# Key norm factors of a cross-attention kernel: turned as two f16 halves and spread over the score layout by a 0/1 matrix, in place of f32 transposes of widened factors

## What is computed

```python
q = (hidden_states @ Wq).reshape(B, Sq, H, D)
k = (encoder_hidden_states @ Wk).reshape(B, Skv, H, D)
v = (encoder_hidden_states @ Wv).reshape(B, Skv, H, D)
q = rmsnorm(q, gq)
k = rmsnorm(k, gk)          # k * rsqrt(mean(k*k) + eps) * gk
scores = jnp.einsum('bqhd,bkhd->bhqk', q, k) * scale
attn = jax.nn.softmax(scores, axis=-1)
out = jnp.einsum('bhqk,bkhd->bqhd', attn, v)
return out.reshape(B, Sq, H * D) @ Wo
```

## Time and profile before

| | |
|---|---|
| median of three runs | 1506.91 us |
| profiled execution | 1508.46 us |
| its span in the trace | 1506.6 us |
| DVE, ACT busy | 987.6 us (66%), 837.5 us (56%) |
| granted TensorE clock, mean | 0.933 |
| DMA | 59.65 MB, mean 40 GB/s |

### The profile page before, as it was taken

One profiled execution on the slowest core, in us unless ns is written; L12 is line 12 of the kernel. 1 busy time (PEld: TensorE's weight loads), 2 busy tenths in 40 slices (PEclk: granted clock), 3 DMA queues, 4 the chain that ended last, 5 costly groups with the idle time before them and its releaser, 6 DMA issues.

```text
span 1506.6 us, 35628 instructions
## 1 busy us (share of the span) xinstructions
PE 1297.3 (86%) x10526; PEld 874.2 (58%) x10526; DVE 987.6 (66%) x3748; ACT 837.5 (56%) x3560; POOL 531.6 (35%) x1337
## 2 busy tenths in 40 slices
PE   5877898999999999989898989899999999955881
PEld 2554565666666666665656656566666666634661
DVE  6754777777677777776767676777767777732212
ACT  4445575747475757566566657575747575711110
POOL 2044152525252533435352515252535243310004
PEclk9998999999999999999999999999999999876996
DMA  9000010101010100000000000010101011002344
GB/s 370 31 23 15 9 30 11 32 11 32 11 32 11 33 11 29 11 26 18 22 21 22 21 8 29 11 32 11 32 11 32 11 32 39 31 3 75 120 153 126
DMA packets 41191, 59.65 MB, mean 40 GB/s; under 512 B 5094, under 2 KB 35953, under 8 KB 40096
## 3 DMA queue, kind: packets, MB, share of 16 engines
q1 hardware_dynamic: 36880, 50.73, 10.6%
q0 software_dynamic: 2064, 6.14, 1.2%
q10 hardware_dynamic: 2176, 2.10, 0.4%
HBM read 48.62 MB, written 10.49 MB: 39 GB/s over the span
## 4 chain that ended last, share of the span: by engine, by line
PE 49%; DVE 21%; issue 9%; POOL 8%; DMA 3%; ACT 3%; POOLq 0%; DVEq 0%; SPq 0%; ACTq 0%
PE AB L594 25%; PE Db L594 9%; PE Eb L594 5%; POOL prob L1177 4%; PE C L719 4%; PE C L594 3%; DVE kst L1312 3%; DVE rq L1360 2%; DMA ctxn<-expert_rows 2%; DVE nc_ L1284 2%; DVE nc_ L1285 2%; DVE nb_ L1286 1%; PE C L787 1%; DVE prob L1471 1%; PE C L734 1%
## 5 line engine op out<-in xcount | busy, mean ns | idle before, releaser
L950 ACT ACTIVATE AB<-AB 128x128 f32<-128x128 f32 (+1 forms) x1160 | 305.3, 263 | 172.8 <-PE AB L594 168.3
L1132 POOL TENSOR_TENSOR pjunk<-pjunk 128x1 f32<-128x1 f32 x288 | 56.1, 195 | 748.4 <-DVE sinv L1482 431.3
L1312 DVE BATCH_NORM_STATS2 kst<-AB 128x6 f32<-128x256 f32 x512 | 181.8, 417 | 68.1 <-PE AB L594 63.0
L950 ACT ACTIVATION_READ_ACCUMULATOR AB<-AB 128x1 f32 (+1 forms) x1160 | 217.3, 187 | 0.0
L594 PE MATMUL AB<-wk_hi,c_hi 128*128 128x512 f16 x512 | 203.7, 398 | 11.9 <-DVE smax L1471 2.9
L594 PE MATMUL AB<-wk_lo,c_hi 128*128 128x512 f16 x512 | 201.3, 393 | 0.0
L594 PE MATMUL AB<-wk_hi,c_lo 128*128 128x512 f16 x512 | 199.7, 390 | 0.0
L1020 ACT ACTIVATE prob<-prob,nbias,rq 128x257 f32<-128x257 f32 x256 | 150.6, 592 | 7.9 <-DVE nbias L1477 7.9
L1177 POOL TENSOR_SCALAR prob<-prob,sinv 128x257 f32<-128x257 f32 x256 | 123.4, 482 | 20.2
L594 PE MATMUL AB<-ctxT,qpT 128*128 128x257 f32 x512 | 124.0, 385 | 0.0
L594 PEld LDWEIGHTS AB<-wk_hi,c_hi 128*128 128x128 f16 x512 | 52.2, 102 | 94.7 <-issue 25.2
(11 more groups left out here) (252 smaller groups left out, 2923.8 us busy)
## 6 DMA issues: line engine op xcount, KB each, us to landing
ctxT<-in_ctxT SPq DMA_DIRECT2D x64, 128.5 KB, 2.1
...
```

Source lines behind the costliest of these rows:

```text
L950: ins = nc.scalar.activation(k, k, ACT.Square, accum_out=sums[0:m, h:h + 1])
L1132: own.mark(pool.tensor_tensor(pjunk[:, 0:1], pjunk[:, 1:2], pjunk[:, 1:2], ALU.mult))
L1312: ins = V.bn_stats(stats[:, 0, 2 * half + n], AB[0:m, 2 + half, 2 * D * n:2 * D * (n + 1)])
```

## The change

The wide buffer `rkx` goes. POOL's new step R_k (k = 0, 1; `split_rk`) waits for KN_k and writes the 64 factors of each context row as an f16 half and the rest as a second f16 half, into `rk16`. PE's new step rt_k (`turn_rk`) turns each of the two blocks by one f16 product with the f16 identity: 64 columns in (sequence, half, head) become 64 partitions. ACT copies them (256 columns) into `rkT`. PE's rk_b is now four products of `spread16[:, b % 2]`, a 64 x 512 matrix of zeros and ones, with `rkT`: both halves are added and every head lands on its 32 partitions. ACT's copy into `rkb` stays. POOL's r_b writes the last column only. `spread16` is built by two DVE operations in step `low` of the first tile. The first tile's one-time widening (`step_rkl`) uses the buffer `sc`; the ternary weights' load and one of the final buffers, which had lain in `rkx`, have other places (`wt_in` of its own, `wvo_words`). The lists of steps change: R and rt come in, and other steps change places as well.

```diff
-    "PE": """K0 pt3 K1 X K2 o3 K3 f Q xt1 rk0 qkv K4 QP s0 qk sc rk1 K5 K6 K7 pv pt0 s1 st pr rk2 s2 o0 xt2 rk3
-              lg up s3 pt1 dn pos o1 pt2 o2""".split(),
-    "ACT": """K0 tl3 K1 X ph3 K2 oh3 K3 Q xt1 rk0 qkv K4 QP qk e0 K5 sc K6 K7 rk1 pv tl0 ph0 rk2 e1 oh0 xt2 rk3 up
-              e2 lg ph1 tl1 e3 oh1 ph2 tl2 oh2""".split(),
-    "DVE": """K0 X K1 XL dp3 K2 do3 K3 KN0 f Q RQ K4 qkv s0 sc i0 K5 sm K6 K7 KN1 ys dp0 yv s1 pr ln2 i1 s2 lg do0
-              up s3 i2 dp1 dn pos do1 dp2 i3 do2""".split(),
-    "POOL": """h0 n3 h3 h1 X c0 cl r1 h2 ln1 c3 r0 n0 c2 r2 c1 y r3 ln2 n1 n2 scat""".split(),
+    "PE": """K0 pt3 K1 X K2 o3 K3 f Q rt0 xt1 rk0 qkv K4 QP s0 qk sc rk1 K5 K6 K7 pv pt0 s1 st rt1 pr rk2 s2 o0
+              xt2 rk3 s3 up lg pt1 dn pos o1 pt2 o2""".split(),
+    "ACT": """K0 ph3 K1 X tl3 K2 oh3 K3 Q rt0 xt1 rk0 qkv K4 QP qk e0 K5 sc K6 K7 rk1 pv ph0 tl0 rt1 rk2 e1 oh0
+              xt2 rk3 up e2 ph1 tl1 lg e3 oh1 ph2 tl2 oh2""".split(),
+    "DVE": """K0 X K1 dp3 XL K2 do3 K3 KN0 f Q RQ K4 qkv s0 sc K5 i0 sm K6 K7 KN1 ys dp0 yv s1 pr ln2 s2 do0 i1 s3
+              up lg i2 dn dp1 pos do1 dp2 i3 do2""".split(),
+    "POOL": """h0 n3 h1 X R0 h3 c2 c0 r0 ln1 h2 c1 n0 r1 cl c3 R1 y r3 ln2 r2 n1 n2 scat""".split(),
...
-    "PE": """KL K0 K1 K2 X K3 rkl Q W0 W1 K4 QP M01 K5 M23 tw rk0 s0 rk1 s1 K6 pt0 K7 pt1 o0 s2 rk2 rk3 s3 o1
-              pt2 o2""".split(),
-    "ACT": """KL K0 wq0 K1 wq1 K2 X K3 rkl Q W0a W0b W1a W1b K4 QP M0a M0b K5 M1a M1b tw rk0 e0 rk1 e1 K6 ph0 tl0
-              K7 ph1 tl1 oh0 rk2 e2 rk3 oh1 e3 ph2 tl2 oh2""".split(),
+    "PE": """KL K0 K1 K2 X K3 rkl Q W0 W1 K4 QP M01 K5 M23 tw rt0 rk0 s0 rk1 s1 K6 pt0 K7 pt1 o0 s2 rt1 rk2 rk3 s3 o1 pt2 o2""".split(),
+    "ACT": """KL K0 wq0 K1 wq1 K2 X K3 rkl Q W0a W0b W1a W1b K4 QP M0a M0b K5 M1a M1b tw rt0 rk0 e0 rk1 e1 K6 ph0 tl0 K7 ph1 tl1 oh0 rt1 rk2 e2 rk3 oh1 e3 ph2 tl2 oh2""".split(),
...
-    "POOL": """hl h1 h3 h2 h0 rkl X r0 r1 cl c0 n0 c1 n1 r2 c2 r3 n2 c3""".split(),
+    "POOL": """hl h1 h3 h2 h0 rkl X R0 r0 r1 cl c0 n0 c1 n1 R1 r2 c2 r3 n2 c3""".split(),
...
-        rkx = sb("rkx", [P, 2, KT, H * SQ])
+        rk16 = sb("rk16", [P, 2, KT, 2, 2, H], F16)
+        rkT = sb("rkT", [BATCH, 2, KT * P], F16)
+        spread16 = sb("spread16", [BATCH, 2, H * SQ], F16)
+        wt_in = sb("wt_in", [P, 10, P])
...
-        rkx_ready = Events(sem("rkx_ready"), pro=["last"] + entries("POOL", PRO, "r"), full=entries("POOL", FULL, "r"))
+        rkl_ready = Events(sem("rkl_ready"), pro=["wide"])
+        rk16_ready = Events(sem("rk16_ready"), pro=["R0", "R1"], full=["R0", "R1"])
+        rkb_last = Events(sem("rkb_last"), pro=entries("POOL", PRO, "r"), full=entries("POOL", FULL, "r"))
...
                 keys(p, "KL", cl_hi, cl_lo, BATCH)
...
             def step_rkl(p):
-                pe.wait_ge(rkx_ready.sem, rkx_ready.at(p, "last"))
+                pe.wait_ge(rkl_ready.sem, rkl_ready.at(p, "wide"))
                 start(p, "rkl")
                 for g in range(G):
-                    ins = pe.transpose(C[:, 0, BATCH * g:BATCH * (g + 1)], rkx[0:BATCH, 0, 0, P * g:P * (g + 1)],
+                    ins = pe.transpose(C[:, 0, BATCH * g:BATCH * (g + 1)], rkl_wide[:, 4 * g:4 * (g + 1)].rearrange("p h q -> p (h q)"),
                                        ident[0:BATCH, 0:BATCH])
                 ins.then_inc(filled["4"].sem, 1)
...
+            def turn_rk(p, k):
+                pe.wait_ge(rk16_ready.sem, rk16_ready.at(p, f"R{k}"))
+                start(p, f"rt{k}")
+                for tt in range(KT):
+                    ins = mm(C[0:BATCH, 0, P * tt:P * (tt + 1)], rk16[:, k, tt].rearrange("p b e h -> p (b e h)"), ident16[:])
+                ins.then_inc(filled["4"].sem, 1)
             def rk_rows(p, b):
...
-                pe.wait_ge(rkx_ready.sem, rkx_ready.at(p, f"r{b}"))
+                pe.wait_ge(drained["4"].sem, drained["4"].at(p, f"rt{b // 2}"))
                 for n, s in enumerate("45"):
                     pe.wait_ge(drained[s].sem, drained[s].turn(p, f"rk{b}"))
                     for g in (2 * n, 2 * n + 1):
-                        for tt in range(KT):
-                            ins = pe.transpose(C[:, n, KT * P * (g % 2) + P * tt:KT * P * (g % 2) + P * (tt + 1)],
-                                               rkx[:, b % 2, tt, P * g:P * (g + 1)], ident)
+                        ins = mm(C[:, n, KT * P * (g % 2):KT * P * (g % 2 + 1)], spread16[:, b % 2, P * g:P * (g + 1)],
+                                 rkT[:, b // 2])
                     ins.then_inc(filled[s].sem, 1)
...
             def scores(p, b):
...
+            steps |= {f"rt{k}": (lambda p, k=k: drain(p, f"rt{k}", "4", rkT[:, k], C[0:BATCH, 0, 0:KT * P])) for k in range(2)}
...
                 pool.tensor_tensor(rstd[:, n:n + 1], var[:, n:n + 1], minus_half[:], ALU.pow)\
                     .then_inc(rstd_ready.sem, 1)
...
-            def spread(p, b):
-                pool.wait_ge(rk_ready.sem, rk_ready.at(p, "KN0" if b < 2 else "KN1"))
+            def split_rk(p, k):
+                pool.wait_ge(rk_ready.sem, rk_ready.at(p, f"KN{k}"))
+                gate()
+                here = rk[:, NB * k:NB * (k + 1)].rearrange("p (b t) h -> p t b h", b=2)
+                own.mark(pool.tensor_copy(rk16[:, k, :, :, 0], here))
+                own.settle()
+                pool.tensor_tensor(rk16[:, k, :, :, 1], here, rk16[:, k, :, :, 0], ALU.subtract).then_inc(rk16_ready.sem, 1)
+            def last_rk(p, b):
+                if b < 2:
+                    pool.wait_ge(rk_ready.sem, rk_ready.at(p, "KN0"))
+                else:
+                    pool.wait_ge(drained["3"].sem, drained["3"].at(p, f"s{b - 2}"))
                 if p.kind == "pro":
                     pool.wait_ge(drained["4"].sem, drained["4"].at(p, "rkl"))
                     pool.wait_ge(start_dve.sem, start_dve.at(p, "wt"))
-                if b >= 2:
-                    for s in "45":
-                        pool.wait_ge(filled[s].sem, filled[s].at(p, f"rk{b - 2}"))
-                    pool.wait_ge(drained["3"].sem, drained["3"].at(p, f"s{b - 2}"))
                 gate()
-                pool.tensor_copy(rkb[:, b % 2, :, SKV - 1:SKV], rk_last[:, :, bass.ds(p.early * NB + b, 1)])
-                for tt in range(KT):
-                    ins = pool.tensor_copy(rkx[:, b % 2, tt].rearrange("p (h q) -> p h q", q=SQ),
-                                           rk[:, KT * b + tt].unsqueeze(2).broadcast_to([P, H, SQ]))
-                ins.then_inc(rkx_ready.sem, 1)
+                pool.tensor_copy(rkb[:, b % 2, :, SKV - 1:SKV], rk_last[:, :, bass.ds(p.early * NB + b, 1)])\
+                    .then_inc(rkb_last.sem, 1)
...
             def normalise(p, b):
...
                 dve.wait_ge(consts_in.sem, consts_in.at(p, "all"))
                 V.tensor_copy(ident16[:], ident)
+                low_high = ident[0:BATCH, 0:BATCH].rearrange("p (b e h) -> p b e h", b=2, e=2)
+                for b in range(2):
+                    V.tensor_tensor(spread16[:, b].rearrange("p (h q) -> p h q", q=SQ),
+                                    low_high[:, b, 0].unsqueeze(2).broadcast_to([BATCH, H, SQ]),
+                                    low_high[:, b, 1].unsqueeze(2).broadcast_to([BATCH, H, SQ]), ALU.add)
                 V.tensor_reduce(low_rows[:], ident[:, G:2 * G], AX.X, ALU.add, negate=True).then_inc(start_dve.sem, 1)
...
             def step_wk(p):
...
-                dve.wait_ge(rkx_ready.sem, rkx_ready.at(p, f"r{b}"))
+                dve.wait_ge(rkb_last.sem, rkb_last.at(p, f"r{b}"))
...
```

More of the change, by code:

```diff
@@ L59 @@
 DVE_STEPS = dict(pro=78, full=85, last=37, expert=0)
-POOL_STEPS = dict(pro=37, full=40, last=5, expert=0)
+POOL_STEPS = dict(pro=41, full=44, last=5, expert=0)
 class Period:
@@ L182 @@
          "dn": "E", "M01": BANKS, "M23": BANKS, "tw": BANKS, "KL": BANKS, "rkl": "4"}
+SLOTS |= {"rt0": "4", "rt1": "4"}
 for _b in range(NB):
@@ L355, in build @@
         wk_in = pxT[:, :, :].rearrange("p h n -> p (h n)")
-        wt_in = rkx[:, :, :, :].rearrange("p a k n -> p (a k n)")[:, 512:512 + 10 * P].rearrange("p (g n) -> p g n", n=P)
+        rkl_wide = sc[0:BATCH]
         wt_b, wt_d = (rkb[:, k].rearrange("p g n -> p (g n)").bitcast(BF16)[:, 0:10 * P].rearrange("p (g n) -> p g n", n=P)
@@ L444, in build @@
         eo = [flat_view(oT[:, 4 * k:4 * k + 4], "p a n", 2) for k in range(2)]
+        wvo_words = wvo_hi[:, :, :].rearrange("p h n -> p (h n)").bitcast(F32).rearrange("p (a c) -> p a c", c=DIM)
         fin = [x[:, :].rearrange("p b n -> p (b n)").rearrange("p (a c) -> p a c", c=DIM) for x in
-               (qpT, rkx[:].rearrange("p a k n -> p (a k) n"))]
+               (qpT, wvo_words)]
         fin = [f[:, 4 * k:4 * k + 4] for f in fin for k in range(2)]
@@ L528, in _ @@
                 sp.dma_start(dst, src).then_inc(weights_in.sem, 16)
-            sp.dma_start(wt_in, d["w_tern"]).then_inc(tern_in.sem, 16)
```

(18 more changed lines are left out.)

## The result

The changed kernel takes 1577.7 us, the middle of 1577.37, 1577.73 and 1583.68, against 1506.83 for the kernel before: a ratio of 1.048 (95% interval 1.045 to 1.051). A fourth execution ran in a slow state (1610.74 us, granted clock 0.824) and is left out of every comparison; with it the median would be 1580.7. The forecast was 1507, with 1489 to 1518 as its range. It was wrong by some 70 us, on the slow side.

A forecast was written before the change was run, and what follows sets the result against it. PE was 86% busy, but waits between engines set part of each tile. A full tile: +0.3 (ln1) - 0.6 (rk1) + 0.2 (tail) = -0.1 us; 15 tiles -1.5, start +2.0, so +0.5 on 1506.91: 1507, range 1489 to 1518.

The forecast's parts named there:

- the tail: From s2 to pt3: pos on DVE late, POOL's scatter waits for slot_s, h0 and n3 later; +0.2 us a tile.
- ln1: POOL's ln1 starts at 468.65 instead of 466.52, making qk late by 0.3 us (0.1 to 0.9) a tile.
- moved steps of POOL: Loads after cl and c0 to c3 wait behind s1 anyway, c3 stays last: worth 0.
- slower rival: POOL late at ln1, overlapped small DVE work stretches; qk 0.9 us late instead of 0.3; 1516 us, chance 0.17.
- rk1: PE behind the qk wait: products save 0.88 us at low clock, K5 may pay half back; gain taken 0.6.
- The clock comes back earlier (rival): Half clock ends before K5, not inside it; 0.64 us a tile, 9.6 in all; 1498 us, chance 0.07.
- rt0 and rk0: PE between Q and QP, ahead of 2.32 us idle before qk: worth nothing either way.
- rt1: PE after st: two products, at most 0.22 us; operand ready as st ends if POOL is free.
- The walk: Step order followed once with the same durations, giving the 1507 case (1500 to 1514); chance 0.42.
- The rival that needed over 5 us: POOL late at ln1, decided if R0 to r0 take over 5 us together; 1516 us, chance 0.17.
- POOL's broad copies: Eight copies a tile at 608 ns go from POOL, which is 35% busy; worth 0 by itself.
- the start: Step low's two DVE operations +1.4 us, rt0 and rt1 uncovered in the first tile; +2.0 us (1 to 3).

The follow-up runs named there:

- e11: Changed kernel plus unread products in three places: seven before the heads wait, five between qk and sc, nine ahead of st; 1515.06 us.
- e12: Changed kernel with cl and c3 ahead of R0 on POOL, plus seven and five unread products around qk; 1501.83 us.
- e13: e12 with dp1 ahead of dn on DVE and ln1 ahead of c2 and c0 on POOL; 1482.11 us.
- e9: Kernel before plus unread products: nine before the heads wait, five between qk and sc; 1481.55 us.
- e8: e1 plus unread products: seven before the heads wait, five between qk and sc; 1479.19 us.
- e1: Changed kernel's new work in the step order of the kernel before, only R0, R1, rt0, rt1 put in; 1505.77 us, ratio 0.999.

## Why the prediction was wrong, step by step

**The sum of it.** With the clock held, the changed kernel is 33.5 us behind the old one (1515.1 less 1481.6). 13.2 of them go with cl and c3 (e11 to e12), 19.7 with the tail and ln1 (e12 to e13), 0.6 is left. These medians also hold what lies outside the full tiles, where the four kernels are at half clock for 96 to 124 us; from the first `qk` to the last, in the profiled executions, the three parts are 17.0, 17.2 and 0.5 us. By steps, a tile of e11 is 2.69 us longer than one of e9: 1.51 from s1 to `st`, 0.12 from `st` to `dn`, 0.90 from `dn` to K2 and 0.48 from Q to `qk`, less 0.33 from `qk` to s1. The ln1 part of the 19.7 (0.46 us a tile) is the price of c3's place in e12, as shown above, and so belongs beside the 13.2.

The rest of the loss is the clock's. It costs the changed kernel 62.6 us (1577.7 less 1515.1) and the old one 27.0 (1508.6 less 1481.6, in the same series): 35.6 more. (33.5 and 35.6 add up to the 69.1 between 1577.7 and 1508.6 by the way they are formed; it is no check.) That the products ahead of `qk` delay nothing else is borne out by the step they stand in: from s0 to `qk` PE takes 3.64 us in e8 and 3.63 in e1, 4.15 in e9 and 4.15 in the kernel before. I had looked for waits only in the places where the steps themselves had changed, and had carried the clock along as it was.

**The step that failed: moved steps of POOL.** The prediction says that cl's and c3's moves are "worth 0". It asked whether anybody waits for their results (nobody does), and whether loads would queue behind them. It did not ask what they run beside. At their new place they stand beside KN1, on the chain to `yred` and `st`: +1.81 us from s1 to `st`. The rows that could have told were there: the xn1 of the earlier trace rows takes 0.60 us beside POOL, and others of its form 0.41. I used 0.60 as that instruction's own length. `px<-px,prec` takes 0.69 us there, but 0.94 at 256.65 us, beside POOL's `cn_lo`. The prediction's slower rival, "small DVE work that overlaps h2 and c1 stretches", had the mechanism, at 0.6 us, in the wrong place.

The Trainium skill (SBUF — State Buffer, "Who interferes with whom") says that a DVE instruction with two SBUF inputs contends with a GpSimd instruction that reads SBUF, that `tensor_scalar` can too, and that whoever issues first holds the shared pair of ports for the whole instruction. The traces agree: `kn` (two inputs) and `nb_` (`tensor_scalar`) end within 0.1 us of POOL's instruction, while the statistics on PSUM (`kst`) take 0.41 us on the mean beside POOL as without it, in the changed kernel. That it is this port, the traces don't show; that it is a wait for the other's instruction to end, they do. One row doesn't go with "whoever issues first": the `xn` of the earlier trace rows starts at 467.12, before this cast of POOL, which keeps its 0.39 us, and it is `xn` that takes 0.60 us in place of 0.41.

```profile
467.18 0.39 POOL L1195 CAST cn_hi<-ctxn 128x256 f16<-128x256 f32 x1
```

By this rule of the Trainium skill and the length of `cl_rows`, 1.15 us, one could have estimated some 1 us for `kn` alone, over half of the 1.8.

**The second that failed: the clock as a constant.** The prediction let half clock cost what it costs now. In fact the 1.8 us of idle time in front of `st` brought a second stretch at 0.50, in which `pr` took 3.6 us rather than 1.9 (3.04 on the mean of 13 tiles); and the first one lasted longer (0.51 in the window after `qk`, in place of 0.83). In all the clock made up 35.6 of the 69 us.

**rk1.** Forecast -0.6 us, half of K5's slow products paying back. In e1 `rk1` fell from 1.76 to 0.83 us and K5 to K7 rose from 10.29 to 11.02; in the changed kernel to 11.22. Nearly all of it was paid back, or more. With the clock up, rk1 goes from 0.93 (e9) to 0.54 (e8). The forecast price of a rk_b was 0.44, from the distance of products inside a long run of them in `f`: it was 0.1 too low, and rk2 saves 0.33 us where 0.43 was counted.

**The clock comes back earlier (rival).** It did not: K5 starts at half clock in e1 as well, though e1 spends 61 us there and not 75. e1 also waits 0.5 us less before `qk`, so that these 14 us can't be laid to products in place of transposes. The rule of the Trainium skill (TensorE: Matmul & The Clock Gate, Part 4: PE-mode transpose), that transposes don't count as PE work, is neither shown nor refuted here.

**rt0 and rk0.** Forecast 0; right. rt0 (0.23 us), xt1 (0.40 more), Q and qkv (0.19 more), less rk0's 0.35, put 0.47 us in front of an idle time that shrank by as much: from s0 to `qk` PE takes 3.63 us in e1 and 4.15 before.

**rt1.** Forecast 0.22 us and ready as `st` ends. It costs 0.59: two products of 0.11, and 0.36 of waiting, for bank "4" holds the turned probabilities of pt0 until DVE's dp0 has drained them (the row at 528.83). I had checked rt1's operand and not its target. The groups behind it also grew: `pr` 1.81 to 1.92, s2 and s3 1.74 to 1.84 each.

**ln1.** The walk gave 4.75 us from R0's gate to ln1. POOL of the changed kernel, R0 and ln1:

```profile
570.13 0.20 POOL L1146 TENSOR_TENSOR pjunk<-pjunk 128x1 f32<-128x1 f32 x1 [12.61 <-DVE rk L1306]
570.26 0.24 POOL L1174 CAST rk<-rk 128x64 f16<-128x64 f32 x1
570.58 0.31 POOL L1176 TENSOR_TENSOR rk<-rk 128x64 f16<-128x64 f32 x1
...
574.85 0.56 POOL L1166 TENSOR_TENSOR rstd<-var,minus_half 128x1 f32<-128x1 f32 x1
```

4.72 us, with the small halves at 0.24 and 0.31 against the estimates of 0.25 and 0.3. `qk` is 0.55 us later than in e1 (4.18 from s0 in place of 3.63), where +0.3 was forecast with 0.1 to 0.9. But beside the kernel before the wait is nearly unchanged (2.31 us for 2.32 in the rows, 2.23 for 2.18 on the mean), since rt0 and xt1 fill what ln1 adds. The rival that needed over 5 us did not happen.

**The tail.** Place right, size wrong: +0.2 forecast, +0.84 measured (e12 less e13, from `dn` to K2). POOL waits for `slot_s` in each of the 12 tiles between 240 and 1250 us, on the mean 0.78 us; here the row behind n2:

```profile
548.24 0.19 POOL L1146 TENSOR_TENSOR pjunk<-pjunk 128x1 f32<-128x1 f32 x1 [0.58 <-DVE slot_s L1649]
```

The length of this wait was in the walk (0.65 us). What failed is its start: I had PE at `dn` 0.8 us earlier. With the steps as measured at full clock in e12, from `st` to `dn`, rk2, rk3 and up save 0.94 us together, and rt1, `pr`, xt2, s2, s3 and pt1 take 1.07 more, so PE comes 0.13 later, and the whole of the new wait is added. It shows at K0, as forecast (0.70 us of idle time where there was none), and little at pt3 (0.38 for 0.18).

**POOL's broad copies, the start.** Copies worth 0: right, POOL is busy 37 us less and nothing follows from it. PE's first product comes at 13.31 us in place of 12.08, +1.2 for the 1.4 forecast, and the first `qk` 1.55 us later, for the 2.0 of the whole start.
